# Tile-by-tile node stages inside the edge passes of a four-layer graph network

## The chip, the cores and the metric

The program runs on one core of one Trainium2 chip, in one launch. The metric is the device time of the run in microseconds (us); lower is better. Three runs of the kernel before gave 9198.25, 9227.61 and 9258.36 us, median 9227.61. One more execution was taken with the hardware profiler; all rows below are from it.

## The reference

There are 6250 nodes with 160 features (64 scalars, 32 vectors of 3 components) and 100000 edges sorted by destination. Four layers follow one another; each normalises the node rows, applies ReLU, and adds a graph convolution to x:

```
h = jnp.maximum(_layernorm(x, axis=-1), 0.0)
x = x + _L0_gnn_ref(h, ...)     # layer 0, and layer 1 in the same form
h = jnp.maximum(_layernorm(x, axis=-1), 0.0)
x = x + _L2_gnn_ref(h, ...)     # attention; its residual is h, with a norm of its own
h = jnp.maximum(_layernorm(x, axis=-1), 0.0)
x = x + _L3_gnn_ref(h, ...)
```

Layers 0, 1 and 3 have one shape. Node maps give a table row for every node. For each edge the row of its source is gathered, a small network on the edge's attributes gives 192 weights (two hidden layers in layer 0, one in 1 and 3), the row is multiplied by weights and by the edge's 4 attributes, and the products are summed over the edges of a destination:

```
outA = wA * xs * y0
outD = wD * jnp.einsum('eud,ed->eu', xv, y1) * INV3
outB = wB[:, :, None] * xs[:, :, None] * y1[:, None, :]
outC = wC[:, :, None] * xv * y0[:, :, None]
agg = jax.ops.segment_sum(edge_feat, edge_dst, num_segments=n)
```

The sums then pass one more linear map. Layer 0 scales the result by a learnt factor of the node; layer 1 rotates between it and a self term, with an angle from the same sums; layer 3 maps twice and scales by node attributes.

## The kernel before, in words

Everything is float32. Nodes lie in 49 tiles of 128 rows, and x stays in SBUF for the whole program. Edges are padded to 196 groups of 512 (four tiles of 128), so there are 4 groups for each node tile. The program is a chain of blocks; each engine has its own queue in each block, and a block ends with a barrier of all engines.

For layers 0, 1 and 3 the blocks are these.

**Node pass** (`node_pass`, lines 343 to 468). Statistics of all 49 tiles on VectorE (line 282), one small square root on ScalarE (line 313), then tile by tile: ReLU of the scaled tile (line 418), two transposes on TensorE (442, 443), two copies out of PSUM (427, 428), two maps (448, 449), a finish on VectorE (`finish_l0` and so on), and a store of the table rows to HBM by SyncE (390). GpSimd clears the buffer of sums, `sums_T` (400). Before layer 2 the pass also makes h and its own norm (lines 292 to 323).

**Edge pass** (`edge_pass`, from line 524). For each group SyncE loads the source indices and attributes (593, 595). GpSimd issues four indirect gathers of 128 rows (606). TensorE computes the hidden layer (624; in layer 0 a second one, 630), the weights (636) and the sums (649). The sums are 20 matmuls of the products against a 40-node window of one-hot columns, accumulated in PSUM. ScalarE applies the activation (664) and multiplies the rows by attribute 0 (672). VectorE makes the one-hot columns and products (697 to 716) and adds the window to `sums_T` (732, after reading the window's first node with a register load). In layers 0 and 1 two half groups share the hidden matmul, with block-diagonal weights: line 636 is two matmuls with 128 rows and 384 columns for a group, one in two of its weights being zero. The gathered rows have four buffers, the PSUM windows and the hidden layers two each. TensorE sums a group three steps after its hidden layer in layer 0, two steps in 1 and 3. If a group of edges spanned 40 nodes or more, the pass would run again with shifted windows (`all_windows`, line 118).

**Post pass** (`post_pass`, lines 736 to 812). For each node tile ScalarE copies the sums (782), TensorE maps them (795, 797), and VectorE adds the result to x (841, 842 in layer 0; 903 to 907 in layer 1; 951, 952 in layer 3). Layer 1 first computes its angles for all nodes, by way of a row in HBM.

Layer 2 runs an attention pass over the same groups (lines 957 to 1414), a softmax, a pass that sums messages (1497 to 1643) and a post pass (1681, 1717). The last block stores x (1740, 1741).

## Time and profile before

| | us |
|---|---|
| median of three runs | 9227.61 |
| lowest and highest run | 9198.25, 9258.36 |
| span of the profiled execution, first to last instruction | 7226.5 |
| layer 0: edge pass | 1013.2 |
| post pass 0 and node pass 1 | 226.6 |
| layer 1: edge pass | 1007.3 |
| post pass 1, node pass 2, start of attention | 305.6 |
| attention | 2610.7 |
| layer 3: edge pass | 1020.5 |
| post pass 3 and last store | 113.2 |

The profile states the span of the profiled execution; no time of that execution from outside the span is given. Between the span and the median of the runs lie 2001 us, which no view of the trace shows. Stage times are lengths of the stretches of one view, cut at the last addition to `sums_T` of a pass and at the first gather of the next. The busy columns count how long an engine had an instruction in it. A float32 matmul leaves two records for each instruction, so counts of matmuls and weight loads are twice those in the code. Consecutive matmul records overlap, so the pace of TensorE is read from starts, not from durations.

### The profile page before, as it was taken

What the parts mean: (1) busy time and instruction counts of PE and PEld (TensorE: products, weight loads), DVE (VectorE), ACT (ScalarE), POOL (GpSimd) and SP (SyncE); (2) the same over time, 40 slices, a digit from 0 to 9 for tenths busy, and PEclk for the clock granted to TensorE, in tenths of its full rate; (3) what the DMA queues carried; (4) which work ended last, traced back from release to release, by engine and by line L of the source; (5) the groups of instructions that cost most, each with busy time, mean ns of one, the idle gap of its engine ahead of it and who ended that gap; (6) DMA issues with size and microseconds to landing.
All of it is one profiled execution on the core that took longest, in us unless ns stands there. A gap on an engine that the chain in (4) does not pass through costs nothing. (4 is left out here: it accounts for less than half of the span.)

```text
span 7226.5 us, 182541 instructions
## 1 busy us (share of the span) xinstructions
PE 6569.0 (91%) x51671; PEld 5175.8 (72%) x51671; DVE 4888.2 (68%) x14416; ACT 3087.1 (43%) x8581; POOL 4427.4 (61%) x3934
## 2 busy tenths in 40 slices
PE   6999999799999857999999999999947879999998
PEld 3777778576666736878878777787836744777777
DVE  4666665476666545777777777777657975666665
ACT  2444443333333344666666666666530012333332
POOL 1777773277777216888877887878720011777772
PEclk9999997599999756889898888989778955999996
DMA  1222221222222213444444444444426701222221
GB/s 61 68 68 68 68 68 34 58 68 68 69 69 68 44 60 61 83 82 83 82 81 80 82 81 81 82 80 83 78 52 174 200 5 36 69 69 69 69 69 44
DMA packets 730807, 526.10 MB, mean 73 GB/s; under 512 B 244683, under 2 KB 677819, under 8 KB 730083
## 3 DMA queue, kind: packets, MB, share of 16 engines
q0 software_dynamic: 263424, 321.38, 22.1%
q1 hardware_dynamic: 467300, 203.73, 11.0%
q8 instruction: 39, 0.64, 0.0%
q14 instruction: 44, 0.36, 0.0%
HBM read 429.13 MB, written 95.55 MB: 73 GB/s over the span
## 5 line engine op out<-in xcount | busy, mean ns | idle before, releaser
L606 POOL DMA_INDIRECT l_edge_g<-node_table,l_edge_idx x2352 | 2281.7, 970 | 1124.3 <-issue 702.9
L649 PEld LDWEIGHTS l_edge_win_ps<-l_edge_hot,l_edge_prod 128*32 128x32 f32 (+2 forms) x23520 | 1515.3, 128 | 247.7 <-issue 170.4
L649 PE MATMUL l_edge_win_ps<-l_edge_hot,l_edge_prod 128*32 128x40 f32 (+2 forms) x23520 | 1620.9, 227 | 4.3 <-DVE sums_T L732 4.3
L1121 POOL DMA_INDIRECT att_g<-node_table,att_ends x784 | 1250.4, 1595 | 238.9 <-issue 238.6
L672 ACT ACTIVATE l_edge_gy<-l_edge_g,y 128x160 f32<-128x160 f32 x2352 | 811.7, 416 | 791.9 <-DMA l_edge_g<-node_table,l_edge_idx 789.3
L1114 POOL DMA_INDIRECT att_g<-node_table,att_ends x784 | 792.8, 1011 | 415.2 <-issue 281.3
L636 PE MATMUL l_edge_w_ps<-l_edge_wo,l_edge_h 128*128 128x384 f32 (+1 forms) x3136 | 907.1, 423 | 0.2 <-ACT l_edge_h L664 0.2
L664 ACT ACTIVATE l_edge_h<-l_edge_h_ps 128x256 f32<-128x256 f32 (+1 forms) x784 | 337.8, 431 | 1126.3 <-PE l_edge_h_ps L624 1076.6
L1141 PE MATMUL att_turn<-ident,sums_T 128*128 128x128 f32 (+1 forms) x4704 | 775.0, 309 | 30.1 <-ACT sums_T L1226 23.7
L636 PEld LDWEIGHTS l_edge_w_ps<-l_edge_wo,l_edge_h 128*128 128x128 f32 (+1 forms) x3136 | 536.8, 191 | 336.1 <-issue 171.7
L1226 ACT ACTIVATE sums_T<-att_turn 128x512 f32<-128x512 f32 (+1 forms) x1176 | 665.3, 591 | 216.7 <-PE att_turn L1141 211.8
L1141 PEld LDWEIGHTS att_turn<-ident,sums_T 128*128 128x128 f32 (+1 forms) x4704 | 572.6, 154 | 205.1 <-issue 119.0
L624 PE MATMUL l_edge_h_ps<-l_edge_ea,l_edge_wi 16*128 16x256 f32 (+1 forms) x1176 | 494.6, 500 | 81.2 <-ACT l_edge_h L664 27.7
L701 DVE TENSOR_TENSOR l_edge_vy<-l_edge_g,y 128x384 f32<-128x384 f32 x588 | 325.9, 554 | 255.5 <-DMA l_edge_g<-node_table,l_edge_idx 254.1
L708 DVE TENSOR_TENSOR l_edge_prod<-l_edge_w_ps,l_edge_g 128x256 f32<-128x256 f32 x588 | 247.9, 422 | 312.7 <-PE l_edge_w_ps L636 312.5
L1216 ACT ACTIVATE att_gy<-att_g,y 128x160 f32<-128x160 f32 x784 | 270.3, 416 | 272.2 <-DMA att_g<-node_table,att_ends 271.7
L703 DVE TENSOR_TENSOR l_edge_hot<-l_edge_hot,y 128x480 f32<-128x480 f32 x588 | 383.2, 652 | 0.0
L1198 PEld LDWEIGHTS att_o<-att_w_o1v,sums_T 128*128 128x128 f32 x1568 | 290.2, 218 | 108.4 <-issue 90.9
L697 DVE TENSOR_TENSOR l_edge_hot<-iota_win,dst_rel 128x160 f32<-128x160 f32 x588 | 192.4, 327 | 253.0 <-PE l_edge_win_ps L649 231.8
L1304 DVE TENSOR_TENSOR att_vec<-att_o,sums_T 128x384 f32<-128x384 f32 x196 | 109.3, 558 | 363.8 <-ACT att_gate L1267 357.3
L1181 PE MATMUL att_o<-att_w_o2s,sums_T 96*128 96x64 f32 x1568 | 334.7, 298 | 10.6 <-ACT sums_T L1226 1.5
L1199 PE MATMUL att_o<-att_w_o1v,sums_T 128*128 128x64 f32 x1568 | 341.3, 304 | 0.0
(232 smaller groups left out, 11533.8 us busy)
## 6 DMA issues: line engine op xcount, KB each, us to landing
l_messages<-att_rows SPq DMA_DIRECT2D x196, 320.0 KB
sum_msg<-l_messages SPq DMA_DIRECT2D x196, 320.0 KB, 3.6
l_edge_g<-node_table,l_edge_idx POOLq DMA_INDIRECT x2352
att_g<-node_table,att_ends POOLq DMA_INDIRECT x1568
node_table<-l_rows SPq DMA_DIRECT2D x245, 80.0 KB, 1.6
att_ea<-in_edge_attr_T SPq DMA_DIRECT2D x196, 64.0 KB
l_scores<-att_score SPq DMA_DIRECT2D x784, 2.0 KB
l_edge_idx<-in_src_groups SPq DMA_DIRECT2D x588, 2.0 KB, 1.7
```

The lines of the kernel that those rows point to most:

```text
L606: pool.indirect_dma_start(g[s][:, t, :], None, rows_of, bass.IndirectOffsetOnAxis(idx[s][:, t:t + 1], 0)).then_inc(fetched[s], 16)
L624: nc.tensor.matmul(h_ps[0][0:HALVES * hid, 0:HC], wi[:, :], ea[s0][:, :]).then_inc(hidden[0], 1)
L636: ins = nc.tensor.matmul(w_ps[s2][:, n * HALVES:(n + 1) * HALVES, 0:wn], h[last][s2][:, n * P:(n + 1) * P], wo[:, :])
L649: ins = nc.tensor.matmul(at, q[:, t, lo:lo + width], to[:, t, kinds, :], start=t == 0, stop=t == TG - 1)
L664: nc.scalar.activation(h[n][s1][:, :], h_ps[n][0:HALVES * hid, 0:HC], act_fn, scale=scales[n]).then_inc(active[n], 1)
L672: ins = nc.scalar.activation(gy[sk % 2][:, t, :], g[sk][:, t, :], ACT.Copy, scale=y4[:, ds((k * TG + t) * 4, 1)])
L703: nc.vector.tensor_tensor(to[:, :, 1:1 + XYZ, :], to[:, :, 0, :].unsqueeze(2).to_broadcast([P, TG, XYZ, EDGE_WIN]), xyz.to_broadcast([P, T ...
L1114: pool.indirect_dma_start(g[s][:, t, :], None, table[2], bass.IndirectOffsetOnAxis(ends[s][:, t:t + 1], 0)).then_inc(fetched[s], 16)
L1121: pool.indirect_dma_start(g[s1][:, t, :], None, table[3], bass.IndirectOffsetOnAxis(ends[s1][:, TG + t:TG + t + 1], 0), compute_op=ALU.add ...
L1141: ins = nc.tensor.transpose(turn[bank][0:width, t * P:(t + 1) * P], f[:, t, at:at + width], ident[:, :])
L1199: ins = nc.tensor.matmul(o1[:, t, PV + VC:O1W], feat_T[0][:, 2, e], w_o1v[1][:, :])
L1226: nc.scalar.activation(feat_T[n][0:width, part, :], turn[bank][0:width, :], ACT.Copy).then_inc(count, 1)
```

## The change

For layers 0, 1 and 3 the stages between the edge passes are moved into the edge pass. The new `edge_stream` runs the 196 groups and after each group calls a `Tail` object on every engine, which may issue one piece of the work of a finished node tile. A tile is ready when 4t+6 groups are added. Its pieces stand at fixed steps: `tile_of(i, s, r, slot, back)` says that the piece comes at step 4(t+back)+slot of that engine's queue. After the last group each engine runs on for 28 steps (layer 0), 32 (layer 1) or 24 (layer 3), which hold only tile work.

Statistics are now taken for one tile at a time. The inverse square root is a power of -0.5 on GpSimd. The four new GpSimd instructions of a tile in layer 1 (two in layer 0, none in layer 3) are on one or two columns of 128 rows and stand in the queue of the gathers. The sine of layer 1 is computed for each tile, between the activations of the edge network. `sums_T` is cleared tile by tile on ScalarE. Results of layer 3 are stored tile by tile. Each tile buffer is single.

To find room in PSUM, the hidden layer and the window of sums have one bank each instead of two. VectorE now adds a window at the start of a step, before the products of that step, and TensorE sums a group two steps after its hidden layer in all layers. The weights matmul becomes four matmuls for a group, of 64 rows (rows 0 to 63 and rows 64 to 127 in turn) and 192 columns, in place of two of 128 rows and 384 columns; the attributes are laid out for it on the host.

The old blocks stay in the program as a second branch (`general`), which runs if a group of edges spans 40 nodes or more, or if a tile's sums could still change after its turn. The setup computes both into `span`.

```diff
+        def tile_of(i, s, r, slot, back):
+            t = r - back
+            return t if s == slot and live(t, NT) else None
+        def ready(t):
+            return min(TG * t + TG + SLACK, NG) if isinstance(t, int) else t * TG + (TG + SLACK)
+        def stream_scale(pool, settled, t, mv, half, scale, bias, rooted):
+            nc.gpsimd.tensor_tensor(scale, mv[:, 1:2], half, ALU.pow).then_inc(rooted, 1)
+            gate(pool, settled, (rooted, 2 * t + 1))
+            nc.gpsimd.tensor_scalar(bias, mv[:, 0:1], scale, -1.0, ALU.mult, ALU.mult).then_inc(rooted, 1)
...
+                            own.pool(pool, i, s, r)
+                            if live(i, NG):
+                                gate(pool, (w_loaded, W_LOAD), (idx_loaded[s], 16 * (r + 1)), (made, (i - 3) * K))
+                                for t in range(TG):
+                                    pool.indirect_dma_start(g[s][:, t, :], None, rows_of, ...)
...
+                            if live(i, NG):
+                                at_least(pe, ea_loaded[s0], 16 * (r0 + 1))
+                                at_least(pe, active[last], i)
+                                nc.tensor.matmul(h_ps[0:HALVES * hid, 0:HC], wi[:, :], ea[s0][:, :]).then_inc(hidden[0], 1)
+                            if live(i - 1, NG):
+                                at_least(pe, active[last], i)
+                                at_least(pe, made, (i - 2) * K)
+                                for n in range(TG // HALVES):
+                                    for m in range(HALVES):
+                                        ins = nc.tensor.matmul(w_ps[s1][:, m * (TG // HALVES) + n, 0:wn],
+                                                               h[last][s1][m * hid:(m + 1) * hid, n * P:(n + 1) * P],
+                                                               wo[m * hid:(m + 1) * hid, :])
+                            if w_mid and live(i, NG):
+                                at_least(pe, active[0], i + 1)
+                                nc.tensor.matmul(h_ps[0:HALVES * hid, 0:HC], wm[:, :], h[0][s % 2][:, :]).then_inc(hidden[1], 1)
+                            if live(i - lag, NG):
+                                at_least(pe, made, (i - lag + 1) * K)
+                                at_least(pe, added, i - lag)
...
+                            own.pe(pe, i, s, r)
...
+                            if live(i - 2, NG):
+                                add_window(dve, i - 2, win_ps, MID, 4, EDGE_WIN, summed, added)
+                            if live(i, NG):
+                                products(i, s, r)
+                            own.dve(dve, i, s, r)
...
+        class TailL0(NodeTail):
+            def pe(self, pe, i, s, r):
+                if (t := tile_of(i, s, r, 3, 4)) is not None:
+                    self.map(pe, t)
+                if (t := tile_of(i, s, r, 1, 3)) is not None:
+                    at_least(pe, self.done, t * self.KD)
+                    self.post_sums(pe, t, 1 + SC, self.w[0:MID, 0:1 + SC], self.w[0:MID, 128:128 + VC])
+                if (t := tile_of(i, s, r, 1, 4)) is not None:
+                    self.turn(pe, t, 1)
...
+            edge_stream("l0", *L0, TailL0, 7)
+            edge_stream("l1", *L1, TailL1, 8)
+            attention_pass()
...
+            layer_3_nodes()
+            edge_stream("l3", *L3, TailL3, 6)
...
+        with nc.If(widest < EDGE_WIN):
+            streamed()
```

TensorE's queue in the loop of layer 0's edge pass: `ea`, `wi` and `h_ps` are the hidden layer, `wo` and `w_ps` the weights, `win_ps` the sums. Before, one step of four:

```order
L624 MATMUL l_edge_h_ps<-l_edge_ea,l_edge_wi 128x256
L64 REGISTER_ALU
L630 MATMUL l_edge_h_ps<-l_edge_h_1,l_edge_wm 128x256
L59 ISA
L636 MATMUL l_edge_w_ps<-l_edge_wo,l_edge_h_0 128x2x192 x2
...
L649 MATMUL l_edge_win_ps<-l_edge_hot,l_edge_prod 96x40 x4
L649 MATMUL l_edge_win_ps<-l_edge_hot,l_edge_prod 64x120 x4
L649 MATMUL l_edge_win_ps<-l_edge_hot,l_edge_prod 32x40 x12
```

Now, the second step of four, with the tile work behind it (`post_ps` the map of the sums, `node_ps` the transposes):

```order
L897 MATMUL l_edge_h_ps<-l_edge_ea,l_edge_wi 128x256
L904 MATMUL l_edge_w_ps<-l_edge_wo,l_edge_h_0 128x192 x4
L60 REGISTER_ALU
L910 MATMUL l_edge_h_ps<-l_edge_h_1,l_edge_wm 128x256
...
L921 MATMUL l_edge_win_ps<-l_edge_hot,l_edge_prod 32x40 x12
...
L1036 MATMUL l_edge_post_ps<-l_tail_w,l_tail_sums 128x65
L1038 MATMUL l_edge_post_ps<-l_tail_w,l_tail_sums 128x32 x3
L60 REGISTER_ALU
L1084 MATMUL l_edge_node_ps<-ident,l_tail_tile 96x128
L1085 MATMUL l_edge_node_ps<-ident,l_tail_tile 64x128
```

The weights of a group now stand ahead of its second hidden layer and are four matmuls, and one step in four carries six matmuls of a node tile (two more, the maps, stand in the fourth step).

GpSimd's queue in the loop of layer 1's edge pass, the gathers of groups in buffers 0 to 2. Before:

```order
L606 DMA l1_edge_g0<-node_table_1,l1_edge_idx0 128x160 x4
L64 ISA
L606 DMA l1_edge_g1<-node_table_1,l1_edge_idx1 128x160 x4
L64 ISA
L606 DMA l1_edge_g2<-node_table_1,l1_edge_idx2 128x160 x4
```

Now, with the two pairs of small instructions of a tile (lines 1286, 1288 for the norm of h, 766, 768 for the norm of x):

```order
L1286 TENSOR_TENSOR l1_tail_scales_h<-l1_tail_v2,l1_tail_half 128x2
L65 REGISTER_ALU
L1288 TENSOR_SCALAR l1_tail_scales_h<-l1_tail_mv_h,l1_tail_scales_h 128x1
L65 ISA
L877 DMA l1_edge_g1<-node_table_1,l1_edge_idx1 128x160 x4
L60 ISA
L766 TENSOR_TENSOR l1_tail_scales<-l1_tail_mv,l1_tail_half 128x1
L65 ISA
L768 TENSOR_SCALAR l1_tail_scales<-l1_tail_mv,l1_tail_scales 128x1
L65 ISA
L877 DMA l1_edge_g2<-node_table_1,l1_edge_idx2 128x160 x4
```

Two of the four gather steps now begin behind a pair of small GpSimd instructions, the second of which waits for the first.

## Rows read from the trace of the kernel before

**Rows 1.** Stretches: length; busy (xcount) of PE, PEld, DVE, ACT, POOL; clock; DMA share; GB/s.

```profile
170.60:1183.80 1013.20, 1012.43 (x9420) 771.64 (x9419) 690.45 (x1959) 421.10 (x1176) 763.62 (x784) 1.00 0.29 67
1183.80:1410.40 226.60, 186.36 (x686) 150.21 (x687) 105.38 (x412) 77.15 (x199) 21.22 (x1) 0.51 0.13 37
1410.40:2417.70 1007.30, 950.07 (x9028) 698.71 (x9028) 679.76 (x1958) 324.65 (x980) 756.45 (x784) 0.99 0.29 67
2417.70:2723.30 305.60, 204.10 (x714) 154.00 (x714) 141.83 (x587) 120.34 (x312) 27.38 (x3) 0.52 0.18 49
2723.30:5334.00 2610.70, 2456.98 (x17652) 2049.28 (x17652) 1910.82 (x5491) 1622.82 (x4509) 2043.10 (x1568) 0.86 0.42 80
...
6092.80:7113.30 1020.50, 1018.18 (x9812) 806.83 (x9812) 685.83 (x1959) 365.55 (x980) 761.59 (x784) 0.99 0.29 67
7113.30:7226.50 113.20, 87.66 (x400) 86.73 (x400) 53.78 (x201) 30.73 (x49) 0.00 (x0) 0.51 0.13 38
```

**Rows 2.** One line in layer 1: the gathers, durations in ns, first and last start.

```profile
L606 POOL DMA_INDIRECT l_edge_g<-node_table,l_edge_idx x784: 942/946/1447, 1410.6 to 2404.6; - x196
```

**Rows 3.** Timeline of TensorE in layer 0: start us, length us, instruction.

```profile
599.85 0.70 PE L630 MATMUL l_edge_h_ps<-l_edge_h,l_edge_wm 128*128 128x256 f32 x2
600.38 1.45 PE L636 MATMUL l_edge_w_ps<-l_edge_wo,l_edge_h 128*128 128x384 f32 x4
601.67 2.74 PE L649 MATMUL l_edge_win_ps<-l_edge_hot,l_edge_prod 128*96 128x40 f32 x40
604.96 0.48 PE L630 MATMUL l_edge_h_ps<-l_edge_h,l_edge_wm 128*128 128x256 f32 x1
```

**Rows 4.** Timeline of TensorE in layer 3, one group.

```profile
6606.35 1.10 PE L624 MATMUL l_edge_h_ps<-l_edge_ea,l_edge_wi 10*100 10x512 f32 x2
6607.37 1.57 PE L636 MATMUL l_edge_w_ps<-l_edge_wo,l_edge_h 100*128 100x192 f32 x8
6608.78 2.74 PE L649 MATMUL l_edge_win_ps<-l_edge_hot,l_edge_prod 128*96 128x40 f32 x40
6611.45 0.67 PE L624 MATMUL l_edge_h_ps<-l_edge_ea,l_edge_wi 10*100 10x512 f32 x1
```

**Rows 5.** Timeline of TensorE in the attention pass.

```profile
4011.53 0.39 PE L1198 MATMUL att_o<-att_w_o1v,sums_T 128*128 128x64 f32 x2
4011.75 0.39 PE L1199 MATMUL att_o<-att_w_o1v,sums_T 128*128 128x64 f32 x2
...
4012.42 0.65 PE L1141 MATMUL att_turn<-ident,sums_T 128*96 128x128 f32 x4
4013.00 1.03 PE L1135 MATMUL att_w_ps<-att_w_rbf,att_ea 16*128 16x224 f32 x8
4013.96 0.33 PE L1141 MATMUL att_turn<-ident,sums_T 128*128 128x128 f32 x1
```

**Rows 6.** Groups by form: busy us, mean ns, idle us before and its releaser.

```profile
L841 DVE SCALAR_TENSOR_TENSOR x<-l_post_ps,l_post_small,x 128x64 f32 x44 | 12.5, 284 | 6.4
L703 DVE TENSOR_TENSOR l_edge_hot<-l_edge_hot,y 128x480 f32<-128x480 f32 x588 | 383.2, 652 | 0.0
L732 DVE TENSOR_TENSOR sums_T<-sums_T,l_edge_win_ps 96x160 f32 x588 | 187.0, 318 | 175.8 <-issue 164.8 <-PE l_edge_win_ps L649 10.0 <-DVE sums_T L732 0.7
```

**Rows 7.** One line: the smallest GpSimd instruction of the trace.

```profile
L1663 POOL IOTA l_post_row_i<- x1: 130/130/130, 5782.0 to 5782.0; 84x1 int32 x1
```

**Rows 8.** Timelines at the ends of the stages.

```profile
1402.08 0.31 DVE L494 TENSOR_SCALAR l_rows<-l_ps_v,l_coef 128x96 f32<-128x96 f32 x1
1410.61 0.95 POOL L606 DMA_INDIRECT l_edge_g<-node_table,l_edge_idx  x1 [113.63 <-DMA l_edge_idx<-in_src_groups]
...
2698.72 0.25 DVE L499 COPY l_rows<-l_ps_v 128x96 f32<-128x96 f32 x1
2723.26 0.97 POOL L1114 DMA_INDIRECT att_g<-node_table,att_ends  x1 [133.61 <-DMA att_ends<-in_dst_groups]
...
7210.77 0.33 DVE L952 SCALAR_TENSOR_TENSOR x<-l_post_ps,l_post_coef,x 128x96 f32<-128x96 f32 x1
```

More of the change, by code:

```diff
@@ L32 @@
 EDGE_WIN, SUM_WIN = 40, 64
+SLACK = 2
 COLS = NPAD + SUM_WIN
@@ L122, in all_windows @@
         sums("", True)
-        widest = nc.values_load(span[0:1, 0:1], min_val=0, max_val=NODES)
         with nc.If(widest >= width):
@@ L158, in setup @@
                 span_f = sbuf(ctx, "span_f", [1, 2 * NG + 1])
+                tile_end = sbuf(ctx, "tile_end", [1, NT - 1], I32)
+                late = sbuf(ctx, "late", [1, NT])
                 ones_row = sbuf(ctx, "ones_row", [1, P])
@@ L574, in edge_pass @@
                 last = layers - 1
-                W_LOAD = 16 * HALVES * len(maps)
+                W_LOAD = 16 * HALVES * (len(blocks) + 1)
                 def half(s, r):
@@ L584, in _ @@
                     def _(sp):
-                        sp.wait_ge(w_zeroed, len(maps))
-                        for w, name in maps:
+                        sp.wait_ge(w_zeroed, len(blocks))
+                        for w, name in blocks:
                             rows, cols = A[name].shape
@@ L589, in _ @@
                                 sp.dma_start(w[n * rows:(n + 1) * rows, n * cols:(n + 1) * cols], A[name]).then_inc(w_loaded, 16)
+                        for n in range(HALVES):
+                            sp.dma_start(wo[n * hid:(n + 1) * hid, :], A[w_out]).then_inc(w_loaded, 16)
                         def step(i, s, r):
@@ L679, in _ @@
                     def _(dve):
-                        for w, _ in maps:
+                        for w, _ in blocks:
                             nc.vector.memset(w[:, :], 0.0).then_inc(w_zeroed, 1)
```

623 lines of the change are left out of this document (586 added, 37 removed).

## The prediction

> **What bounds the kernel now.** I read the stretches of the span first [rows 1]. Each edge pass takes 1007 to 1020 us for 196 groups. In layers 0 and 3 TensorE is busy all of it, in layer 1 it is free for 57 of 1007 us; VectorE is busy for 68%, ScalarE for 32 to 42%. The three stretches that the change moves take 226.6 + 305.6 + 113.2 = 645.4 us, at a granted clock of 0.51 to 0.52 (the 1.2 GHz level), where the edge passes have 0.99 to 1.00 (2.4 GHz). They are chains of short steps in which each engine waits for the next: in the first, VectorE is busy 105 us of 226.6.
>
> The second thing to read is the pace of a group, engine by engine, since moved work is paid by what sets that pace. GpSimd in layer 1: from the first gather to the last, (2404.6 - 1410.6) / 783 = 1.27 us from start to start, of which 0.94 are work and 0.33 lie between two [rows 2]; four gathers, 5.08 us a group. TensorE in layer 0, by starts: second hidden layer 0.53, weights 1.29, sums and first hidden layer 3.29, together 5.11 [rows 3]. In layer 3: hidden layer 1.02, weights 1.41, sums 2.67, together 5.10 [rows 4]. So two engines run at nearly the same pace in layers 0 and 3, and GpSimd leads in layer 1. VectorE is busy 679.76 / 196 = 3.47 us a group there [rows 1]. Whatever is added to GpSimd shows in full; what is added to TensorE shows where it isn't paid for by the change of the weights.
>
> **What goes and what stays of the 645.4 us.** The tile work that comes before the last groups lies beside them. The tiles that become ready after the last group, and the hand-over, stay.
> - After layer 0: the last two or three tiles on single buffers, with the engines at the lower clock. Old tile work ran at 226.6 / 49 = 4.6 us a tile for both passes; three tiles and a last chain of about 7 us make some 18 us as an estimate, bounds 10 and 40. Then the hand-over from the last table row to the first gather, 1402.08 to 1410.61 = 8 us [rows 8].
> - After layer 1: a tile has twice the chain (sums map, rotation, two norms, maps), so 35 us, the same bounds. Attention then starts as before, 2698.72 to 2723.26 = 25 us [rows 8].
> - After layer 3: short tiles, 10 us; the last store and the end, 7210.77 to 7226.5 = 16 us [rows 8].
>
> That is 112 us. Weight loads of the tile work and two waits at the start of the passes, which queue ahead of index loads on SyncE, are taken as 5 us in layers 1 and 3 each: 122 us. Removed: 645 - 122 = 523 us.
>
> **What each group grows by.**
> - Weights matmul: eight matmul records of 16 rows and 224 columns, in row groups, took 0.96 us from start to start of what follows, 4013.00 to 4013.96 [rows 5]. By columns the new four (also eight records, 192 columns) would take 192/224 of it, 0.82; I take 0.85 against 1.29 in layer 0, a gain of 0.44. The bounds are 0.65, half of the old time, and 1.41, what the same eight records of 192 columns took in layer 3 without row groups [rows 4]. I go by the row that has the row groups. Layer 3 has a hidden layer of 100 rows; two halves don't fit into 128, its weights stay as they are, and nothing is gained.
> - TensorE's tile work: a 64-column matmul starts 0.22 after the one before, and four records of transposes span 0.58 [rows 5]. In layer 0 a tile has four matmuls of the sums (4 x 0.22 = 0.9), two transposes (0.6 at most), two maps of 96 and 128 columns (0.65 as an estimate, between two 64-column matmuls and their double), with 0.2 for waits: 2.3 us, or 0.58 a group. TensorE then needs 5.11 - 0.44 + 0.58 = 5.25 in layer 0. Layer 1 has no second hidden layer: 5.25 - 0.53 = 4.72. In layer 3 a tile has no norm and no maps for a table, 0.96 us, so 5.10 + 0.24 = 5.34.
> - GpSimd's: two small instructions a tile in layer 0, four in layer 1. The trace has no power on GpSimd; its smallest instruction takes 0.13 us [rows 7]. With the 0.33 that lies between two gathers I take 0.46 each, since these operands are as small. The bounds are 0, if they fit in that gap, and 1.27, the pitch of a gather [rows 2]. A group gets 2 x 0.46 / 4 = 0.23 in layer 0 and 0.46 in layer 1: 5.31 and 5.54. The inputs they wait for are made two or three groups earlier, so the wait itself should cost nothing; were it not so, the gathers have four buffers, and a late piece delays the group four steps on.
> - VectorE's: an instruction on 64 columns takes 0.28 us, with 6.4 / 44 = 0.15 us of waiting ahead of it where the one before feeds it; a window's addition has 164.8 / 588 = 0.28 us ahead of it, and now stands at the start of the step [rows 6]. In layer 1 a tile has about 20 instructions, some of them chained, 6.5 us: 3.47 + 0.28 + 1.64 = 5.4 us a group, just under GpSimd. In layer 0 and 3 it stays below 4.9.
> - ScalarE has the copies, the clearing of `sums_T`, and the sine of layer 1; at 32 to 42% busy [rows 1] it has 3 us a group free, and nothing waits for it but TensorE's next hidden layer. With one hidden bank TensorE's step waits for the activation, with the weights now between. I cost all of it at nothing; without that cover the activation would show with a few tenths of a us a group. SyncE's stores of a tile stand behind index loads that run four groups ahead: nothing.
>
> Layer 0 becomes the larger of 5.25 and 5.31, a growth of 0.20 x 196 = 39 us over 5.11. Layer 1: 5.55, as two engines are nearly equal there, 0.47 x 196 = 92 over 5.08. Layer 3: 5.34 against 5.10 or 5.11, 0.23 x 196 = 45. In all 176 us.
>
> The sum is 176 - 523 = -347 us: the span goes from 7226.5 to about 6880. The profiled execution's own time beside its span isn't given; the median of the runs, 9227.6, is 2001 us above the span. I take these as constant, so 9228 - 347, about **8880 us**.
>
> **The rivals.**
> - *Forecast, 0.52.* With other sizes of the drains and of TensorE's part, 8800 to 8950.
> - *Small instructions are dear in layer 1, 0.16.* Each GpSimd instruction costs up to a gather's pitch: layer 0 at 5.08 + 0.63 = 5.71, +118, layer 1 at 5.08 + 1.27 = 6.35, +249. With layer 3's 45 the growth is 412, and the time 9228 - 523 + 412 = 9117; half way, 9000. For it: GpSimd leaves 0.33 us between two gathers although nothing is awaited [rows 2], and VectorE has almost no room in layer 1. Against: the 0.13 of [rows 7].
> - *Time outside the span shrinks with it, 0.08.* At 9228 / 7226.5 = 1.277 the saving is 347 x 1.277 = 443, giving 8785. No row tells.
> - *VectorE and GpSimd wait for each other, 0.09.* The gathers take 942 ns at least and 946 in the mean while VectorE works [rows 2], so they aren't held up; but they compute nothing. A GpSimd instruction that reads SBUF could meet the 0.65 us products of two SBUF operands, line 703 [rows 6], with a wait of its length before each: 0.5 x 0.65 more for each of 2 and 4 a tile gives 0.16 and 0.33 a group, 96 us, and if each of the pair waits a whole one 192. Time 8976 to 9072. The Trainium skill, "SBUF — State Buffer", section "Who interferes with whom", says that "a DVE instruction with two SBUF inputs contends with a GpSimd instruction that reads SBUF", and calls the lock exclusive. No row here shows it, as GpSimd has no compute instruction beside VectorE's in an edge pass.
> - *TensorE's clock falls, 0.06.* The attention pass, with more kinds of short matmuls and waits, has 0.86 [rows 1]. At that, layer 0 needs 5.25 / 0.86 = 6.1 and layer 3 5.34 / 0.86 = 6.2: 0.8 and 0.85 a group over the forecast, 155 + 167 us, about 9200, no change. Against: the edge passes keep 0.99 at 94% busy or more; but attention is 94% busy too (2457 of 2610.7), so the row doesn't exclude it.
> - *One bank for the window of sums makes the two engines take turns, 0.05: slower.* VectorE must add window i before TensorE may begin the next sums. If the sums (2.67) also had to wait for the products of that step (3.5 and the 0.3 of the addition), a group would take 2.67 + 3.5 = 6.2 us. Then 9228 - 523 + (6.2 - 5.1) x 588 = 9352. It decides from a growth of 523 / 588 = 0.89 a group, a period of 6.0. Against: the products of a group are made a step before its sums, so the two should lie beside each other, with about 2 us of room.
>
> That the change does nothing of what it says is left out: the widest group spans 36 nodes here, under 40, so the new branch runs. The remaining 0.04 is for a cause I don't see, of either sign.
>
> **How the numbers follow.** The time is the forecast's. The range, 8700 to 9120, has the third case's 8785 in it with 80 us for smaller drains and free GpSimd instructions, and goes up to the dear end of the second; above it lie the clock, the turns and what I don't see. Less than 1% from before, 9135 to 9320, is about what a measurement of this kernel can't tell from no change. Faster by more: forecast, second to fourth case and most of the last, 0.88. Within: the clock and a little of the others, 0.07. Slower: 0.05.
>
> **What the profile will show.** Right: stretches of about 1052, 1099 and 1066 us at a clock of 0.99 or more, with 31, 60 and 26 us behind them; the weights' four matmuls at 0.85 us a group; gathers at 1.27 us still, and a further 0.46 for each small GpSimd instruction. Wrong: a clock under 0.95, a GpSimd pair that takes over 1.5 us, VectorE over 95% busy in layer 1, sums that wait for `sums_T`, or drains over 40 us. The forecast itself fails if a pass grows by more than 0.6 us a group.

## The result: slower by 2.7%, and two levels of the kernel before

The change took 9475.78 us (median of 4 runs, 9431.36 to 9506.61) against 9231.56 for the kernel before: ratio 1.0269, 95% interval 1.0223 to 1.0314. The forecast was 8880 us, range 8700 to 9120. It was wrong in sign.

The stretches of the profile of the change, cut as in [rows 1] (same columns; the six are layer 0, the gap, layer 1, the gap to attention, layer 3, the end):

```profile
172.20:2068.30 1896.10, 1399.75 (x10847) 1088.25 (x10846) 725.01 (x2199) 492.62 (x1451) 813.31 (x876) 0.71 0.17 40
2068.30:2092.00 23.70, 11.26 (x46) 7.62 (x45) 4.19 (x18) 8.52 (x20) 2.44 (x6) 0.59 0.12 34
2092.00:3834.80 1742.80, 1384.49 (x10450) 1076.80 (x10450) 814.66 (x2831) 464.00 (x1388) 876.97 (x966) 0.68 0.19 46
3834.80:3884.20 49.40, 15.73 (x53) 9.94 (x52) 13.42 (x78) 11.63 (x33) 6.32 (x14) 0.52 0.24 74
7877.70:9443.60 1565.90, 1329.31 (x10193) 1050.31 (x10192) 695.06 (x2056) 390.17 (x1027) 784.71 (x784) 0.79 0.20 47
9443.60:9456.70 13.10, 2.71 (x21) 2.30 (x20) 2.30 (x6) 1.26 (x2) 0.00 (x0) 0.69 0.09 24
```

The gaps are as short as forecast. The passes aren't 1050 to 1100 us but 1566 to 1896, at a granted clock of 0.68 to 0.79. Against [rows 1] that would be 2230 us more, where the runs differ by 244. The stages of layer 2 between the last gap and layer 3, whose code is the same, are longer too: 3993.5 us, where [rows 1] have 3369.5. So the two profiles can't be compared: the span of the change, 9456.7, is its run time, and the 7226.5 of [rows 1] is not the 9228 of the kernel before. A second profile of the kernel before, taken beside its timed runs, has a span of 9237.9:

```profile
170.50:1593.40 1422.90, 1219.05 (x9420) 883.08 (x9419) 680.03 (x1959) 392.61 (x1176) 778.11 (x784) 0.87 0.20 48
1593.40:1819.40 226.00, 186.63 (x687) 150.49 (x688) 105.11 (x412) 77.15 (x199) 21.23 (x2) 0.51 0.13 37
1819.40:3280.50 1461.10, 1194.67 (x9028) 845.76 (x9027) 673.55 (x1959) 328.63 (x980) 766.24 (x784) 0.82 0.20 47
3280.50:3585.40 304.90, 203.47 (x714) 153.87 (x714) 141.50 (x587) 120.37 (x312) 27.34 (x2) 0.52 0.18 49
7605.30:9125.20 1519.90, 1391.68 (x9812) 1081.08 (x9811) 677.69 (x1959) 366.40 (x980) 781.41 (x784) 0.73 0.19 45
9125.20:9237.90 112.70, 87.60 (x400) 86.68 (x400) 53.54 (x201) 30.76 (x49) 0.00 (x0) 0.51 0.13 38
```

The stages between are as in [rows 1], to the microsecond; the edge passes are 40 to 50% longer. A job is one set of timed runs, of the kernel before and of one or more others beside it. The kernel before has two levels, and every timed execution of a job has the same: **lower**, 7201 to 7211 us in five jobs, and **upper**, 9209, 9232 and 9436 us in three. Only the first profile, of [rows 1], differs from the timed runs that it was recorded with; whether it was taken on the same device isn't recorded. The records name the device of one upper and of one lower job by the same number, 4, so the number doesn't settle it; what sets the level is open. The change wins at one and loses at the other:

| | before | change | ratio (interval) |
|---|---|---|---|
| upper | 9209 | 9500 | 1.0320 (1.0267 to 1.0373) |
| lower | 7201 | 6983 | 0.9691 (0.9650 to 0.9732) |

**Where the time went, upper level** (the two blocks above, after minus before): layer 0 +473, gap -202, layer 1 +282, gap -256, layer 3 +46, end -100, all else -25: together +219. At the lower level (below) the passes grow by 109, 183 and 43 us. So what the upper level adds is 364 us in layer 0, 99 in layer 1 and 3 in layer 3.

In layer 0 TensorE is idle for 1896.1 - 1399.8 = 496 us against 204, and busy for 181 us more, in part because more of its work is done at half clock. The clock records of the two traces give how often the clock fell to 0.50 (1.2 GHz) in a pass, and for how long in all:

| | before | change |
|---|---|---|
| layer 0 | 59 times, 379 us | 54 times, 1082 us |
| layer 1 | 69 times, 536 us | 59 times, 1131 us |
| layer 3 | 44 times, 816 us | 60 times, 670 us |

In layers 0 and 1 the clock doesn't fall more often in the change; it stays down two to three times as long (20.0 us at a time in layer 0, against 6.4).

**What a hold-up looks like.** TensorE in layer 0 of the kernel before, upper level (start, length, instruction, idle before it):

```profile
808.27 1.55 PE L649 MATMUL l_edge_win_ps<-l_edge_hot,l_edge_prod 128*96 128x40 f32 x14
...
813.10 0.29 PE L649 MATMUL l_edge_win_ps<-l_edge_hot,l_edge_prod 128*32 128x40 f32 x2 [1.13 <-issue]
...
814.55 1.18 PE L649 MATMUL l_edge_win_ps<-l_edge_hot,l_edge_prod 128*32 128x40 f32 x15 [0.51 <-issue]
815.67 1.21 PE L624 MATMUL l_edge_h_ps<-l_edge_ea,l_edge_wi 16*128 16x256 f32 x2
```

and the clock around it:

```profile
808.00:813.00 5.00, 2.86 (x24) 2.08 (x23) 0.00 (x0) 0.00 (x0) 3.79 (x4) 0.97 0.26 66
813.00:819.00 6.00, 4.96 (x24) 3.24 (x24) 4.90 (x14) 3.23 (x11) 1.46 (x2) 0.50 0.09 20
819.00:827.00 8.00, 7.67 (x63) 5.49 (x61) 1.94 (x6) 0.73 (x3) 6.17 (x7) 0.96 0.27 68
```

In the midst of the sums, whose operands are all there, TensorE starts single matmuls with pauses that nothing releases ("issue"). VectorE's last product of that group ended at 806.04. Sums of 2.67 us (that length by starts in [rows 4]) take 7.4 (808.27 to 815.67); the clock is at 0.50 for some 6 us from 813 on. GpSimd goes on meanwhile. Code loading isn't the cause in layer 0: the instruction queues move no packet between 253 and 1573 us of this trace. What holds TensorE up is open. Now the change, layer 0:

```profile
1056.25 0.69 PE L897 MATMUL l_edge_h_ps<-l_edge_ea,l_edge_wi 16*128 16x256 f32 x2
...
1065.14 0.38 ACT L935 ACTIVATE l_edge_h<-l_edge_h_ps 128x256 f32<-128x256 f32 x1 [11.85 <-remote]
1065.19 0.33 SPq L860 DMA_DIRECT2D l_edge_ea<-in_edge_attr_T  x1
...
1065.57 1.22 PE L910 MATMUL l_edge_h_ps<-l_edge_h,l_edge_wm 128*128 128x256 f32 x2 [7.78 <-issue]
```

```profile
1058.00:1065.00 7.00, 0.00 (x0) 0.00 (x0) 1.81 (x5) 0.00 (x0) 5.38 (x6) 0.55 0.29 68
1065.00:1072.00 7.00, 6.43 (x43) 5.67 (x44) 1.62 (x5) 3.40 (x9) 2.27 (x3) 0.50 0.25 64
```

The first hidden layer's record ends at 1056.94, but ScalarE and SyncE, which both wait for its semaphore, go on only at 1065.14 and 1065.19. Ends of matmul records are modelled; by its waiters its result came 8 us later. In the kernel before a step's second hidden layer is that of the previous group (`live(i - 1, NG)` there, `live(i, NG)` now). With one bank for the hidden layers it needs ScalarE's result of the same step, so TensorE stands empty, and then works at 0.50 for 7 us and more.

### The profile page after: what moved, and what is told of

It reads as the page before. It is cut to its first block and busy times, and to the rows that moved or that the text cites. A ratio compares the mean times of both kernels' runs of the same rounds, so it can differ in the third digit from the quotient of the medians.

```text
span 9456.7 us, 183998 instructions
## 1 busy us (share of the span) xinstructions
PE 7719.1 (82%) x53213; PEld 6153.1 (65%) x53213; DVE 4796.8 (51%) x14528; ACT 3145.4 (33%) x8806; POOL 4557.7 (48%) x4226
## 5 line engine op out<-in xcount | busy, mean ns | idle before, releaser
L921 PE MATMUL l_edge_win_ps<-l_edge_hot,l_edge_prod 128*32 128x40 f32 (+2 forms) x23520 | 2285.1, 266 | 743.4 <-issue 503.3
L921 PEld LDWEIGHTS l_edge_win_ps<-l_edge_hot,l_edge_prod 128*32 128x32 f32 (+2 forms) x23520 | 2060.2, 161 | 1063.9 <-issue 976.4
L751 DVE TENSOR_TENSOR sums_T<-sums_T,l_edge_win_ps 96x160 f32 x588 | 187.0, 318 | 2163.6 <-remote 928.7
L1821 PE MATMUL att_turn<-ident,sums_T 128*128 128x128 f32 (+1 forms) x4704 | 940.6, 357 | 207.6 <-issue 89.8
L1821 PEld LDWEIGHTS att_turn<-ident,sums_T 128*128 128x128 f32 (+1 forms) x4704 | 708.1, 180 | 407.2 <-issue 220.9
L904 PE MATMUL l_edge_w_ps<-l_edge_wo,l_edge_h 64*128 64x192 f32 (+1 forms) x4704 | 878.7, 413 | 70.6 <-issue 69.0
L904 PEld LDWEIGHTS l_edge_w_ps<-l_edge_wo,l_edge_h 64*128 64x128 f32 (+1 forms) x4704 | 629.7, 227 | 453.3 <-issue 424.3
L897 PE MATMUL l_edge_h_ps<-l_edge_ea,l_edge_wi 16*128 16x256 f32 (+1 forms) x1176 | 591.6, 583 | 79.8 <-issue 40.2
L1861 PE MATMUL att_o<-att_w_o2s,sums_T 96*128 96x64 f32 x1568 | 406.7, 352 | 17.3 <-ACT sums_T L1906 15.0
L1862 PE MATMUL att_o<-att_w_o2v,sums_T 128*128 128x64 f32 x1568 | 401.7, 349 | 0.0
L1863 PE MATMUL att_o<-att_w_o2v,sums_T 128*128 128x64 f32 x1568 | 400.0, 348 | 0.0
```

The lines of the kernel that those rows point to most:

```text
L897: nc.tensor.matmul(h_ps[0:HALVES * hid, 0:HC], wi[:, :], ea[s0][:, :]).then_inc(hidden[0], 1)
L904: ins = nc.tensor.matmul(w_ps[s1][:, m * (TG // HALVES) + n, 0:wn], h[last][s1][m * hid:(m + 1) * hid, n * P:(n + 1) * P], wo[m * hid:(m + ...
L921: ins = nc.tensor.matmul(at, q[:, t, lo:lo + width], to[:, t, kinds, :], start=t == 0, stop=t == TG - 1)
L1821: ins = nc.tensor.transpose(turn[bank][0:width, t * P:(t + 1) * P], f[:, t, at:at + width], ident[:, :])
L1861: nc.tensor.matmul(o2[:, t, 0:SC], feat_T[1][0:MID, 0, e], w_o2s[:, :])
L1862: nc.tensor.matmul(o2[:, t, Q2:PV2 + VC], feat_T[1][:, 1, e], w_o2v[0][:, :])
```

## The experiments

Each kernel was timed beside the kernel before. The expectations name three theories for the loss at the upper level: A, the 64-row weights; B, the single banks; C, the tile work between the groups. A figure "a group" is the pace of the gathers, from the first start to the last of a pass.

**The kernel before and the change again** (no edit). 

> The kernel before, unchanged, profiled a second time. The first profile has a span of 7226.5 us at a mean granted clock of 0.872, while its timed runs took 9198 to 9258 us; the profile of the change has a span of 9456.7 us (clock 0.726) that equals its timed run. Theory T (TensorE is held up in bursts and its clock falls to 0.5 after each, in both kernels, and the first profile happened to be of an execution without them): span about 9200 us, clock 0.70 to 0.78, edge groups of 7 to 8 us instead of 5.1, attention near 3200 us. Rival U (the 2001 us lie outside the span): span again 7200 to 7300 us at a clock of 0.87, time 9230 us.

> The change, unchanged, profiled on the same chip as the kernel before. Theory T: span within 1% of 9457 us, groups of 9.5, 8.8 and 7.9 us in layers 0, 1 and 3 as in its first profile, with bursts of TensorE stalls. Rival V (the first profile of the change fell in a bad execution as the one of the kernel before in a good one): some executions have a span below 7500 us and groups near 5.3 us.

Measured: 9236 us, span 9237.9, clock 0.748; groups of 7.17, 7.38 and 7.61 us. The change took 9500 us, with groups of 9.64, 8.72 and 7.94. T holds; U and V fall. In the timed runs the 2001 us lie inside the span.

**Weights back to wide** in the change (both passes, with the old layout of attributes):

```diff
-    for m in range(HALVES):
-        ins = nc.tensor.matmul(w_ps[s1][:, m * (TG // HALVES) + n, 0:wn],
-                               h[last][s1][m * hid:(m + 1) * hid, n * P:(n + 1) * P], wo[m * hid:(m + 1) * hid, :])
+    ins = nc.tensor.matmul(w_ps[s1][:, n * HALVES:(n + 1) * HALVES, 0:wn], h[last][s1][:, n * P:(n + 1) * P], wo[:, :])
```

> The change with one part undone: the weights are again two matmuls of 128 rows and 384 columns with a block-diagonal matrix; stream, tiles, single banks stay. Groups in the second profiles: before 7.2, 7.4, 7.6 us (layers 0, 1, 3), the change 9.6, 8.7, 7.9. Theory A (the 64-row matmuls in turns are what TensorE is held up by): 7.6 and 7.8 us in layers 0 and 1, 7.9 in 3, time near 8880 us. Theory B (single banks, fewer steps between the hidden layers and the sums): as the change, 9.5 and 8.7 us, about 9480 us. Theory C (the tiles' matmuls between the groups): also as the change or 0.4 us a group longer, 9480 to 9650 us.

**64-row weights alone** (the reverse edit, in the kernel before). 

> The kernel before with one part of the change alone: four weights matmuls of 64 rows and 192 columns instead of two of 128 rows and 384 columns in layers 0 and 1; nothing else. Theory A: groups go from 7.2 and 7.4 us to about 9 and 8.5 us, time 9700 to 9850 us; layer 3 stays at 7.6. Theories B and C: no slower than before, and up to 0.44 us a group faster, 9060 to 9230 us.

**The new loop without tiles:**

```diff
-            edge_stream("l0", *L0, TailL0, 7)
+            edge_stream("l0", *L0, NoTail, 1)    # every method of NoTail is empty
+            post_l0()
+            node_pass("l1", ...)
...
```

> The change without the tile work inside the passes: the new loop (single banks, sums two steps behind, addition first, 64-row weights), and the stages between as blocks of their own as before. Theory A: groups of 9 and 8.5 us in layers 0 and 1, time 9700 to 9900 us. Theory B: the same, and layer 3 slower than 7.6 too. Theory C: 7.2, 7.4, 7.6 us, time 9150 to 9250 us.

**New stream in layer 3 alone** (layers 0 and 1 run the old blocks). 

> Blocks, edge passes and weights of the kernel before in layers 0 and 1; the new stream with its tiles in layer 3 alone, whose weights matmuls are the same in both kernels. All theories: layer 3's groups at 7.9 us instead of 7.6 (196 x 0.3 = 60 us more), the last stretch 13 to 26 us instead of 113 (about 90 less): within 0.5% of the kernel before, about 9200 us. It tells how much of the change pays where the weights aren't touched.

The job came at the lower level, 7209 us, so it says nothing about A, B and C. Ratios: wide weights 0.9681 (0.9645 to 0.9718), 64-row alone 1.0009 (0.9991 to 1.0028), loop without tiles 1.0009 (0.9991 to 1.0027), layer 3 alone 0.9952 (0.9938 to 0.9966). At this level the weights and the loop change little by themselves (the loop costs 0.1% here and 0.3% in the next job); layer 3 alone gains 0.5%, though its groups grew to 5.36 us, 48 us in all.

**The same in a second job**, with the change: 

> The change itself once more, with the kernel before beside it, since chips differ: on one the kernel before takes 9209 us, on another 7209 us. Theory D (the change pays where TensorE runs without hold-ups and costs where it is held up): if the kernel before takes near 7200 us here, the change takes 6850 to 6950 us (passes near 1050, 1110 and 1067 us); if it takes near 9200, the change takes 9440 to 9520. Rival E (the change is slower anywhere): 7200 us or more where the kernel before takes 7200.

> The change with the weights as two matmuls of 128 rows and 384 columns again. Where the kernel before takes 7200 us: 6976 us as measured there (groups 5.66, 5.92, 5.36 us). Where it takes 9200: by theory A (the 64-row matmuls in turns are what TensorE is held up by) groups of 7.7 and 7.9 us in layers 0 and 1 in place of 9.6 and 8.7, time 8900 us; by theories B and C (single banks; the tiles' matmuls) 9.5 us or more and 8.7 or more, 9480 to 9650 us.

> The change without its tile work in the passes (64-row weights, single banks). Where the kernel before takes 7200 us: 7222 us as measured there. Where it takes 9200: theory A 9 and 8.5 us a group in layers 0 and 1 and 9700 to 9900 us; theory B the same, with layer 3 above 7.6 too; theory C 7.2, 7.4 and 7.6 us and 9200 us.

Lower level again, 7201 us: the change 0.9691, wide weights 0.9679 (0.9654 to 0.9704), no tiles 1.0026 (1.0011 to 1.0042). Theory D holds in sign (6983 us, where it said 6850 to 6950, with passes of 1122 and 1191 us for 1050 and 1110); E falls. The stretches of the change at this level:

```profile
172.40:1294.80 1122.40, 1080.61 (x10845) 856.54 (x10845) 724.44 (x2199) 498.81 (x1451) 819.30 (x876) 0.96 0.27 67
1294.80:1319.60 24.80, 13.58 (x48) 9.91 (x48) 4.16 (x18) 8.42 (x20) 2.45 (x6) 0.50 0.11 32
1319.60:2510.20 1190.60, 1096.99 (x10447) 874.53 (x10448) 817.15 (x2831) 466.23 (x1388) 882.47 (x966) 0.85 0.27 67
2510.20:2560.50 50.30, 16.88 (x55) 10.91 (x54) 13.46 (x78) 11.65 (x33) 6.36 (x15) 0.50 0.23 73
5889.80:6953.70 1063.90, 1061.16 (x10193) 848.38 (x10192) 700.66 (x2056) 390.43 (x1027) 779.02 (x784) 0.99 0.28 69
6953.70:6966.80 13.10, 2.75 (x21) 2.33 (x20) 2.33 (x7) 1.26 (x2) 0.00 (x0) 0.69 0.08 24
```

These may be set against [rows 1], which is of this level. Layer 0 grew by 109 us, layer 1 by 183, layer 3 by 43. GpSimd in layer 0 shows a large part of why:

```profile
809.54 0.96 POOL L877 DMA_INDIRECT l_edge_g<-node_table,l_edge_idx  x1 [0.30 <-issue]
810.52 0.58 POOL L766 TENSOR_TENSOR l_tail_scales<-l_tail_mv,l_tail_half 128x1 f32<-128x1 f32 x1
811.28 0.27 POOL L768 TENSOR_SCALAR l_tail_scales<-l_tail_mv,l_tail_scales 128x1 f32<-128x1 f32 x1 [0.18 <-POOL l_tail_scales L766]
812.13 1.02 POOL L877 DMA_INDIRECT l_edge_g<-node_table,l_edge_idx  x1 [0.58 <-issue]
```

Gather to gather over a pair is 2.59 us (the middle value of 45 as well) where 1.27 is usual [rows 2]: 1.32 for the pair, where 0.92 was forecast. The pairs make 0.33 us a group, and the gathers, whose mean went from 974 to 992 ns, another 0.07. That leaves some 0.16 of layer 0's 0.56; TensorE's clock was at 0.96 there.

**Half the small GpSimd instructions moved:**

```diff
-            nc.gpsimd.tensor_scalar(bias, mv[:, 0:1], scale, -1.0, ALU.mult, ALU.mult).then_inc(rooted, 1)
+            nc.vector.tensor_scalar(bias, mv, scale, -1.0, ALU.mult, ALU.mult).then_inc(rooted, 1)   # two steps or more later, in VectorE's queue
```

> The change, with one of each pair of small GpSimd instructions moved to VectorE (the bias of the norm; the power stays on GpSimd): one small GpSimd instruction a tile in layer 0 instead of two, two in layer 1 instead of four. The kernel before has been measured at two levels, near 7200 and near 9220 us. At 7200, the change had groups of 5.65, 6.0 and 5.34 us in layers 0, 1 and 3, against 5.11, 5.06 and 5.10. If GpSimd's queue sets the pace there (theory G), half of layer 0's growth goes, 5.40 us, and a part of layer 1's, 5.7 to 5.85: time 6880 to 6930 instead of 6983 us. If other waits set it (single banks, VectorE: theory H), no change or longer, 6980 to 7050. At 9220: the gathers wait for the rest there, so no change by either, 9440 to 9520.

> The change with wide weights matmuls once more, for the second level of the kernel before. Near 7200 us: 6970 us as measured twice. Near 9220 us: by theory A (the 64-row matmuls in turns are what TensorE is held up by) groups of 7.7 and 7.9 us in layers 0 and 1 instead of 9.6 and 8.7, time near 8900 us; by theories B and C (single banks; the tiles' matmuls) 9.5 and 8.7 us or more, 9480 to 9650 us.

Lower level, 7207 us: the edit took 6858 us, ratio 0.9506 (0.9489 to 0.9522), better than expected; wide weights alone 0.9651. Groups of 5.37 us in layer 0 and 5.65 in layer 1 (before the edit 5.67 and 6.00). G holds, H falls. The power that is left, in layer 0:

```profile
819.06 0.95 POOL L880 DMA_INDIRECT l_edge_g<-node_table,l_edge_idx  x1 [0.30 <-DVE l_edge_prod L986]
820.03 0.58 POOL L766 TENSOR_TENSOR l_tail_scales<-l_tail_mv,l_tail_half 128x1 f32<-128x1 f32 x1
820.78 0.99 POOL L880 DMA_INDIRECT l_edge_g<-node_table,l_edge_idx  x1 [0.17 <-issue]
```

Gather to gather over it is 1.72 us: alone it costs 0.45 to 0.47, as forecast. So the dear one of a pair is the second, which waits for the first: 1.32 less 0.46 is 0.86. At one a tile that makes 0.22 us a group of the 0.30 that layer 0 gained; with the edit the clock there is at 0.99 instead of 0.96.

**Both edits.** 

> The change with both edits together: wide weights matmuls, and one of each pair of small GpSimd instructions on VectorE. Where the kernel before takes 7200 us: 6840 to 6880 us (the GpSimd edit alone gave 6858). Where it takes near 9220 us, a group of the change takes 9.6, 8.8 and 7.9 us in layers 0, 1, 3, in part at half clock: theory A (the 64-row matmuls leave TensorE less busy, so that its clock stays down longer after a hold-up) 7.7 and 7.9 us in layers 0 and 1, time 8850 to 8950 us; theories B (single banks) and C (the tiles' matmuls) above 9 and 8.5 us, 9350 us or more.

**The new loop, wide weights, no tiles.** 

> The new loop with wide weights and without tile work; the stages between are blocks as before. It differs from the kernel before by the single banks, the order of addition and products, and the lag of the sums. Where the kernel before takes 7200 us: 7210 to 7230 us. Where it takes near 9220 us: theory B 9 us a group or more in layer 0 and above 8 in 1 and 3, time 9700 us or more; theories A and C 7.2 to 7.6 us, time 9200 to 9300 us.

Lower level, 7208 us: both edits 0.9543 (0.9514 to 0.9573), the loop without tiles 1.0022 (1.0006 to 1.0038). The edits don't add up. Layers 0 and 1 with half of GpSimd's, 64-row weights, then with wide ones:

```profile
172.20:1235.00 1062.80, 1044.84 (x10846) 826.39 (x10845) 731.74 (x2245) 502.05 (x1451) 807.22 (x830) 0.99 0.28 71
1258.40:2380.60 1122.20, 1044.71 (x10447) 836.31 (x10448) 826.97 (x2921) 473.79 (x1387) 856.75 (x875) 0.89 0.28 71
```

```profile
172.70:1297.30 1124.60, 1116.92 (x10064) 849.77 (x10063) 731.19 (x2245) 506.91 (x1451) 826.37 (x830) 1.00 0.28 67
1320.70:2413.70 1093.00, 1049.55 (x9663) 774.64 (x9664) 837.55 (x2921) 459.39 (x1387) 840.73 (x875) 0.99 0.30 73
```

In layer 0 wide weights fill TensorE (busy 1116.9 of 1124.6) and cost 62 us. In layer 1, where TensorE has room, the 64-row weights leave it at a clock of 0.89 and the wide ones at 0.99, and the pass is 29 us shorter.

**A pause in TensorE's queue**, in the kernel before and the change:

```diff
+                            if s == 0 and not isinstance(i, int):
+                                with pe.Fori(0, 24):
+                                    pass
```

> The kernel before with a pause in TensorE's queue once every four groups in the edge passes: an empty loop of 24 turns, some 6 to 7 us by the 0.2 us branch and the 0.1 us that lie beside it. It imitates one hold-up per turn of the loop on a device that has none. Near 7200 us for the kernel before: a turn takes 20.4 us plus 5 to 7 of the pause plus 2 to 5 at half clock: groups of 7 to 8 us, time 8400 to 8900 us. Theory A (after a pause the change stays at half clock for longer, for its 64-row weights leave TensorE less busy): 6 to 8 us at half clock per pause here.

> The change with the same pause in its three passes. Theory A: 15 us or more at half clock per pause in layers 0 and 1, groups of 8.5 to 9.5 us there, and the gain over the kernel before (218 us without pauses) is lost or turns into a loss: time at least 100 us over that of the kernel before with its pauses. Rival I (a pause costs both the same, and the loss at the second level comes from more or longer hold-ups): the change with pauses stays 100 to 300 us faster than the kernel before with pauses.

> The change with wide weights and half the small GpSimd instructions, again without a pause, as the level of comparison in this job and for the second level of the kernel before should it come up: 6880 us where the kernel before takes 7200; where it takes 9220, theory A 8900, theories B and C 9350 us or more.

Lower level, 7211 us. The kernel before with 141 pauses (47 turns of the loop, three layers) took 9016 us, 12.8 for each, above the 8400 to 8900 expected. The change with 120 (40 turns) took 8427 us, or 12.0 for each above 0.9691 x 7211. The third, without pauses, took 6868 us. In layer 0 of the kernel before one pause is:

```profile
814.00:823.00 9.00, 0.44 (x13) 0.32 (x9) 1.69 (x5) 0.00 (x0) 4.16 (x5) 0.64 0.19 47
823.00:831.00 8.00, 7.89 (x34) 5.56 (x35) 1.94 (x6) 2.05 (x6) 0.51 (x1) 0.55 0.02 2
```

These are 9 us of nothing and then some 8 at half clock. Taken together an equal pause costs the change no more, so the loss that theory A forecast didn't come. By pass it isn't so even: a pause added 11.4, 10.4 and 18.0 us to layers 0, 1 and 3 of the kernel before, and 12.7, 8.5 and 15.1 to those of the change; in layer 0 the clock stayed down for 18.8 us at a time in the change and 11.4 in the kernel before, in layer 1 for 13.3 in both. So layer 0 shows a little of what theory A says, layers 1 and 3 nothing of it. A pause between two groups isn't a hold-up within the sums, and doesn't settle what makes the latter dearer.

**Wide weights in layer 1 only, 64 rows in layer 0, half of GpSimd's,** beside the loop without tiles. 

> The change with one of each pair of small GpSimd instructions on VectorE, 64-row weights in layer 0 and wide weights in layer 1. Where the kernel before takes 7200 us: layer 0 as with the GpSimd edit alone (5.37 us a group, against 5.66 with wide weights), layer 1 as with wide weights (5.50 against 5.65), layer 3 5.34: 6820 to 6840 us, below both kernels and all versions so far. Where it takes near 9220 us: if the 64-row weights are what makes hold-ups dearer, layer 1's groups at 7.4 to 7.9 us instead of 8.8 while layer 0 stays at 9.6, time near 9260; otherwise 8.7 us or more in layer 1 and 9440 us.

> The new loop with wide weights and no tile work, a second time. Where the kernel before takes 7200 us: 7220 us as measured. Where it takes 9220: if the single banks make hold-ups dearer, 9 us a group or more in layer 0 and above 8 in 1 and 3, time 9700 us or more; if not, 7.2 to 7.6 us and 9200 to 9300 us.

This job came at the upper level, 9436 us: with tiles 9550 us, ratio 1.0108 (1.0063 to 1.0153), without 9588 us, 1.0143 (1.0092 to 1.0195). Both are slower than the kernel before, by less than 2%. The loop without tiles, then with them; layers 0 and 1 (layer 3 took 1567.7 and 1623.3 us):

```profile
172.90:1724.90 1552.00, 1230.09 (x9420) 910.98 (x9419) 662.69 (x1959) 399.49 (x1176) 770.24 (x784) 0.84 0.19 44
1959.90:3460.60 1500.70, 1180.96 (x9028) 858.45 (x9027) 666.73 (x1959) 325.98 (x980) 775.60 (x784) 0.80 0.20 45
```

```profile
172.20:2012.20 1840.00, 1281.79 (x10847) 1014.49 (x10847) 735.97 (x2245) 495.89 (x1451) 798.37 (x830) 0.75 0.17 41
2035.80:3745.00 1709.20, 1372.88 (x9666) 994.66 (x9666) 831.10 (x2921) 469.40 (x1387) 838.43 (x875) 0.75 0.20 46
```

The tile work adds 288, 209 and 56 us, 552 in all, against 44, 85 and 44 = 173 for the same pairs at the lower level (loop without tiles 1019.0, 1007.8 and 1019.8 us; with them 1062.8, 1093.0 and 1063.9). Layer 0's share has the step from wide to 64-row weights in it, at both levels. The 552 us use up the 563 us of stages that the tile work removes (235.0 to 23.6, 303.1 to 51.3, 113.3 to 13.2). In layer 1, with wide weights in both, the clock fell 68 times without tiles and 59 times with them, and stayed down for 8.7 and 14.3 us at a time: the tile work by itself lengthens the half clock. Layer 1 with wide weights still takes 8.56 us a group, not 7.4 to 7.9: the weights aren't the main cause. C is the largest of the three, with a share for B: the loop alone costs 1.4% at this level and 0.1 to 0.3% at the lower one, though less than B had it (7.82 us a group in layer 0, where B said 9 or more). No profile of the kernel before was kept in this job, so the 1.4% isn't split by layer. What TensorE waits for in layer 0 (total us, times, longest), all at the upper level: the kernel before, the loop without tiles, this job's version with tiles, and the change itself:

```profile
PE l_edge_win_ps L649 <- issue: 184.2, 241, 2.6
...
PE l_edge_h_ps L630 <- issue: 1.4, 2, 0.8
```

```profile
PE l_edge_h_ps L911 <- ACT l_edge_h L936: 197.3, 50, 6.4
...
PE l_edge_h_ps L911 <- issue: 51.0, 14, 5.1
```

```profile
PE l_edge_h_ps L917 <- ACT l_edge_h L942: 382.7, 41, 12.3
PE l_edge_h_ps L917 <- issue: 80.6, 13, 11.5
```

```profile
PE l_edge_win_ps L921 <- issue: 264.9, 246, 3.3
PE l_edge_h_ps L910 <- issue: 97.0, 30, 9.2
PE l_edge_h_ps L910 <- ACT l_edge_h L935: 83.8, 17, 13.6
```

Before, the hold-up lies in the sums. With one hidden bank much of it comes up at the second hidden layer, which waits for ScalarE and so for TensorE's own late end (the 7.78 us shown above stand as "issue"): 248 us without tiles, 463 with them, and 181 in the change itself, against 1.4. The 181 us are the larger part of the 292 us by which TensorE's idle time grew there; the waits in the sums grew too, from 184 to 265 us. In the two other versions those are 52 and 73 us, so where the hold-ups come up differs from version to version. That layers 1 and 3, with no second hidden layer, have so little of the upper level's extra cost (99 and 3 us of 466) speaks for the same; no run with two hidden banks beside the tiles tests it. GpSimd's small instructions wait 652 us for VectorE in this pass, but VectorE waits only 14 us for gathered rows, so the gathers aren't what is late.

## Why the prediction was wrong

- **The step that failed** is the last of the sum, "I take these as constant". The 2001 us between span and median weren't outside the span. They were hold-ups of TensorE and half clock inside the edge passes and layer 2, in every timed run and not in the one profile: the second profile's span, 9237.9 us, is its run's time less 1.9. The whole sum was made at the lower level and the timing at the upper, where the three passes grow by 801 us and not by 176. A ratio of run time to span of 1.28 should have been the first rival, as "the profile is not of the timed condition"; my rival on it only scaled the saving, and kept its sign.
- **The cover of ScalarE** was costed at nothing: "nothing waits for it but TensorE's next hidden layer", "with the weights now between". At the lower level that is right (TensorE waits 5.8 us in all for ScalarE in layer 0). At the upper the wait at the second hidden layer is 181 us in the change, and 248 and 463 in the two other versions.
- **What was removed**: the stretches that stay were put at 122 us and are 24.8 + 50.3 + 13.1 = 88. (Three tiles at 4.6 us and a chain of 7 would be 21 us, not the 18 that the prediction took.)
- **Growth at the lower level**: 176 us forecast, 336 measured. Layer 3's 45 were 43. TensorE's tile work in layer 0, 0.58 a group, was 0.55 (5.66 with wide weights, which fill TensorE, against 5.11). The mis-sized term was the small GpSimd instruction: 0.46 forecast for each, 0.66 measured in the mean of a pair. A first one at 0.46 was right; it is the second, dependent one that costs 0.86. Layer 0 grew by 0.56 a group, not 0.20, layer 1 by 0.92, not 0.47. Moving half of them gave back 0.30 and 0.35. At this level the second rival, at half its price (9000 - 9228 = -228 us), is about what happened: -218. In part that is luck: its growth, 294 us, was 336, and 557 us were removed and not 523. The prediction calls the gathers' 946 ns their mean; it is the middle value, and the mean of layer 1 is 965.
- **VectorE and GpSimd waiting for each other** does occur. The powers hardly show it (549 ns at least, 584 in the middle of 98), but the second instruction of a pair does, at the lower level in layer 1:

```profile
1790.57 0.84 POOL L768 TENSOR_SCALAR l_tail_scales<-l_tail_mv,l_tail_scales 128x1 f32<-128x1 f32 x1 [0.17 <-POOL l_tail_scales L766]
1790.70 0.65 DVE L978 TENSOR_TENSOR l_edge_hot<-l_edge_hot,y 128x480 f32<-128x480 f32 x1
```

It takes 0.26 to 0.27 us where VectorE is idle, and 0.84 here, ending some 0.05 us after a VectorE instruction with two SBUF operands; 31 of this trace's 147 second instructions took over 0.30 us. This agrees with the lock that the Trainium skill, "SBUF — State Buffer", section "Who interferes with whom", describes. The rival's price was far too high: the excess of the 147 is some 10 us in all, where it had 96 to 192.

- **The clock** did fall, to 0.68 to 0.79 in the passes. At the upper level it falls with the hold-ups, in the kernel before too. At the lower level it fell to 0.96 in layer 0 of the change and to 0.85 in layer 1, and there the form of the weights matters (0.89 against 0.99): a part of this rival is true.
- **Turns of the two engines** was the one rival that said slower, and its 9352 us is the nearest to 9476. That is luck: the loop without tiles holds 5.1 us a group at the lower level, so the turns didn't occur.
- **Open**: what sets the level and what a hold-up is; why tile work keeps the clock down for longer and costs three times as much at the upper level; and how the GpSimd edit and layer 1's weights share the 1.6 to 2.1% between the change and its last version there. Wide weights in both layers with the tiles, and the GpSimd edit alone, were never timed at the upper level. None of the three versions timed there (the change among them) beats the kernel before; at the lower, the change with half the small GpSimd instructions does by 4.9%.

## What to carry to other kernels

Compare the profile's span with the timed runs before anything else. Here every profile with a time of its own had a span 2 to 5 us below it; the first, 2001 us below the median of the timed runs, was of another condition, and a forecast from it holds for that condition alone. A step that sends TensorE's result to another engine and back within the same step cost 6 us in a pass while TensorE was steady and 181 to 463 when it wasn't; a step of distance and two banks would be the thing to try where the queue may be held up (not tried here). A small instruction in GpSimd's queue of gathers costs far more than its work: here 0.46 us for a power on one column, and 0.86 for a second one that waits for it, so move the dependent one first.

## What the hardware showed that I had not expected

- TensorE can be held up with all operands there: sums of 2.67 us took 7.4, with 59 falls of the clock in the 1423 us of layer 0. The same kernel took 7201 us in every execution of one job and 9209 in those of another. Chains of short steps at half clock aren't touched (226.0 against 226.6 us).
- A semaphore of a matmul came 8 us after the end that its record shows; ScalarE and SyncE, released together, tell the true end.
- A pause of some 9 us without matmuls cost 12.8 us on average: 4 more than itself, in the half clock that followed.
- A GpSimd instruction of 0.27 us took 0.84 beside VectorE's products of two SBUF operands.
